# The eight-head attention layer of a graph network: four of a chunk's 64 gathers made by one-hot products on TensorE, and the end chunk in a free part of a buffer

## What is computed

```python
def _gat_conv(x, W, att_src, att_dst, bias, src, dst, heads, out_ch, concat):
    n = x.shape[0]
    h = (x @ W).reshape(n, heads, out_ch)
    a_src = jnp.einsum('nhc,hc->nh', h, att_src)
    a_dst = jnp.einsum('nhc,hc->nh', h, att_dst)
    logits = jax.nn.leaky_relu(a_src[src] + a_dst[dst], NEG_SLOPE)
    m = jax.ops.segment_max(logits, dst, num_segments=n)
    e = jnp.exp(logits - m[dst])
    denom = jax.ops.segment_sum(e, dst, num_segments=n)
    alpha = e / denom[dst]
    msgs = h[src] * alpha[:, :, None]
    out = jax.ops.segment_sum(msgs, dst, num_segments=n)
    out = out.reshape(n, heads * out_ch) if concat else out.mean(axis=1)
    return out + bias
loops = jnp.arange(N, dtype=edge_index.dtype)
src = jnp.concatenate([edge_index[0], loops])
dst = jnp.concatenate([edge_index[1], loops])
h = x @ W_map + b_map
h = _gat_conv(h, W1, att_src1, att_dst1, b1, src, dst, heads=8, out_ch=8, concat=True)
```

## Time and profile before

| | us |
|---|---|
| median of 3 runs | 3327.02 (3321.53 to 3329.48) |
| the profiled execution | 3327.11 |
| its span, first to last instruction | 3325.3 |
| the stretch of `edge_chunks`, first gather to last join | 2396.6 to 3010.8 |
| POOL, busy in the whole span | 970.5 |
| TensorE, granted clock over the span | 0.899 |

### The profile page before, as it was taken

How to read it: one execution, slowest core, us unless ns; L and a number is a source line. 1 busy time by engine, 2 the same in 40 slices (tenths; PEclk the granted TensorE clock), 3 DMA queues, 4 the chain that set the end, 5 groups by cost and what they waited for, 6 DMA issues and landing times. The chain is left out here.

```text
span 3325.3 us, 42240 instructions
## 1 busy us (share of the span) xinstructions
PE 2793.2 (84%) x14474; PEld 2097.3 (63%) x14474; DVE 1770.5 (53%) x4020; ACT 1383.9 (42%) x2629; POOL 970.5 (29%) x785
## 2 busy tenths in 40 slices
PE   5778887999996999999999999999864444456997
PEld 3445774777775877878877787785423333344775
DVE  8998657999967541121122121112664444447994
ACT  4573235999995221121111111111333333333896
POOL 6110070000001632213322222230277777750000
PEclk9999897999998999999999999999756666666999
DMA  5334442111002522212211213110211111113200
GB/s 161 137 112 151 180 163 89 41 55 70 1 1 95 197 102 86 76 58 89 94 60 70 88 65 125 60 65 7 74 31 29 29 29 29 29 20 129 80 36 20
DMA packets 73828, 252.16 MB, mean 76 GB/s; under 512 B 20459, under 2 KB 52784, under 8 KB 63920
## 3 DMA queue, kind: packets, MB, share of 16 engines
q1 hardware_dynamic: 56728, 222.19, 17.7%
q0 software_dynamic: 16896, 27.27, 3.8%
HBM read 218.24 MB, written 31.17 MB: 75 GB/s over the span
## 5 line engine op out<-in xcount | busy, mean ns | idle before, releaser
L2961 PE MATMUL psum<-gate_stream,parts 128*128 128x384 f32 (+1 forms) x3600 | 668.9, 344 | 8.6 <-ACT x L3001 4.4
L2961 PEld LDWEIGHTS psum<-gate_stream,parts 128*128 128x128 f32 x3600 | 631.6, 189 | 25.5 <-issue 6.1
L3066 POOL CAST gate_stream<-gate_adj 128x1920 fp32r<-128x1920 f16 (+1 forms) x200 | 372.2, 1868 | 836.2 <-PE psum L2961 826.4
L2321 PE MATMUL psum<-gat_h,gat_pair 128*128 128x129 f32 (+1 forms) x3750 | 571.1, 292 | 10.4 <-DVE gat_pair L2125 9.5
L2321 PEld LDWEIGHTS psum<-gat_h,gat_pair 128*128 128x128 f32 (+1 forms) x3750 | 460.9, 190 | 126.2 <-issue 77.7
L1637 POOL DMA_INDIRECT edge_rows<-edge_table,src_idx x440 | 436.4, 992 | 184.8 <-issue 133.5
L3099 DVE SCALAR_TENSOR_TENSOR gate_work<-psum,bhh,gate_work 128x384 f32<-128x384 f32 (+1 forms) x80 | 50.1, 626 | 780.8 <-PE psum L2908 763.1
L2125 DVE SCALAR_TENSOR_TENSOR gat_pair<-gat_above,gat_adj 128x512 f32<-128x512 f32 (+3 forms) x525 | 328.7, 626 | 87.4 <-PE psum L2321 58.0
L2234 ACT ACTIVATE gat_above<-psum,gat_as 128x512 f32<-128x512 f32 (+3 forms) x525 | 329.4, 627 | 42.9 <-PE psum L2309 41.2
L2225 ACT ACTIVATE psum<-gat_ad_rows,gat_as 128x512 f32<-128x512 f32 (+3 forms) x525 | 334.9, 638 | 16.9
L2080 DVE SCALAR_TENSOR_TENSOR gat_acc<-gat_adj,gat_q,gat_acc 128x512 f32<-128x512 f16 (+3 forms) x497 | 330.7, 683 | 0.0
(11 more groups left out here) (497 smaller groups left out, 3918.9 us busy)
## 6 DMA issues: line engine op xcount, KB each, us to landing
gate_adj<-adj SPq DMA_DIRECT2D x35, 2400.0 KB, 8.1
gat_adj<-adj SPq DMA_DIRECT2D x8, 3200.0 KB, 11.0
gcn_adj<-adj SPq DMA_DIRECT2D x10, 2400.0 KB, 8.5
adj<-count_stage SPq DMA_DIRECT2D x196, 100.0 KB, 1.7
gate_adj<-adj SPq DMA_DIRECT2D x5, 2800.0 KB, 9.0
edge_rows<-edge_table,src_idx POOLq DMA_INDIRECT x440, 2.5
gcn_adj<-adj SPq DMA_DIRECT2D x2, 3200.0 KB, 10.2
gcn_adj<-adj SPq DMA_DIRECT2D x2, 2800.0 KB, 10.0
```

Source lines behind the costliest of these rows:

```text
L2321: mm = e.matmul(ps[0:p, b, a:a + D + 1], pair[:, g % 2, i * P:i * P + p], h1[:, hi, h, :], start=hi == 0 and i % 3 == 0, stop=hi == NT - 1 ...
L2961: mm = e.matmul(ps[:, f, 0:hi - lo], parts[:, t, m, f, :], stream[:, (NGG * i + t // GG) % GR, 0:windows(i), t % GG * W:(t % GG + 1) * W], ...
L3066: e.tensor_copy(stream[:, n % GR, 0:windows(i), :], cols[:, i % 2, 0:windows(i), g * GW:(g + 1) * GW]).then_inc(widened, 1)
```

## The change

For the six chunks of 64 steps, the last four steps are no longer gathered by POOL (DRAWN): POOL has 60 gathers in these chunks and 416 in all. The four steps (a **batch**) come from PE. ACT and DVE first split the 72 numbers of each node into three bf16 parts (`parts`, 216 columns for a tile). A second scratch in HBM holds the source indices in f16, read back as `src_rows`. For each batch PE spreads the source indices over the partitions (`sources`), ACT copies them to f16 (`lay`), DVE compares them with the node numbers of each of the 25 tiles (`find`, ring of 12 buffers), PE adds up 4 products for each tile (`pull`, 216 columns, f16 one-hot and bf16 parts, PSUM banks 6 and 7), and DVE adds the three parts into `edge_rows` (`draw`, two reductions). The batch of chunk 0 stands ahead of all look-ups. The batch of chunk c + 1 stands among the sums of chunk c: from the fifth step on, every second `keep_busy` product gives way to the 4 products of one tile; on DVE `find` and `draw` follow the weighting of chunk c.

The end chunk uses rows 32 to 55 of side 0 and of `edge_hot`, which chunk 6 (32 steps) leaves free, and no longer waits for a chunk's sums. Every `widen` has one `keep_busy` product ahead of it. `masked`, `logit`, `top`, `part`, `fwd` and `bwd` lie in tiles that are free at that time. Clearing the banks (now L2004) stands behind the maximum's transposes (now L1994), and the small products are in bank 4 in place of bank 7. Some semaphores are merged.

```diff
+DRAWN = (4, 4, 4, 4, 4, 4, 0, 0)
+NSRC = NP // 2 - 32
+RING = 12
...
+        e.dma_start(self.k.src_scratch.rearrange("(j p q) -> p j q", j=KJ, p=KP), self.sf[:]).then_inc(self.kept, 16)
...
+        e.tensor_scalar(self.sf[:], part(0), -float(NSRC), None, ALU.add)
...
+        free_g = spare_g[:].rearrange("p t w -> p (t w)")
+        masked, logit, top = (free_g[:, n * KP * HEADS:(n + 1) * KP * HEADS].rearrange("p (s h) -> p s h", h=HEADS) for n in range(3))
+        part = spare_t[:, 0:NT * SUMS].rearrange("p (t w) -> p t w", w=SUMS)
+        fwd, bwd = (spare_t[:, NP - (n + 1) * tiles * P:NP - n * tiles * P].rearrange("p (i q) -> p i q", q=P) for n in range(2))
...
+        by_pool = [size[c] - DRAWN[c] for c in range(end + 1)]
+        batches = [(c, s) for c in range(end + 1) for s in range(by_pool[c], size[c], EG)]
+        of_chunk = [[m for m, (k, _) in enumerate(batches) if k == c] for c in range(end + 1)] + [[], []]
...
+        side = [c % 2 for c in range(end)] + [0]
+        base = [0] * end + [size[end - 1]]
+        row = lambda c: rows[:, side[c], base[c]:base[c] + size[c], :]
+        arrival = side[:end] + [2]
+        landed = [16 * sum(by_pool[k] for k in range(c + 1) if arrival[k] == arrival[c]) for c in range(end + 1)]
+        hot_of = lambda c: hot[:, base[c]:base[c] + size[c], :]
...
-                    if c >= 2:
+                    if 2 <= c < end:
                         e.wait_ge(summed, c - 1)
-                    for s in range(size[c]):
+                    for s in range(by_pool[c]):
...
+                def find(share):
+                    for m, lo, hi in share:
+                        if lo == 0:
+                            e.wait_ge(src_in, m + 1)
+                        for t in range(lo, hi):
+                            n = m * NT + t
+                            if n >= RING:
+                                e.wait_ge(pulled, n - RING + 1)
+                            e.tensor_scalar(one[:, n % RING, :], src_wide[:, m % 2, :], self.tile_ids[:, t:t + 1], None,
+                                            ALU.is_equal).then_inc(ones, 1)
+                def draw(m):
+                    c, s = batches[m]
+                    e.wait_ge(pulled, (m + 1) * NT)
+                    if 2 <= c:
+                        e.wait_ge(summed, min(c - 1, end - 2))
+                    for j in range(2):
+                        of = ps[:, 6 + j, 0:6 * ROWS].rearrange("p (s n w) -> p s w n", n=3, w=ROWS)
+                        inst = e.tensor_reduce(row(c)[:, s + 2 * j:s + 2 * j + 2, 0:ROWS], of, AX.X, ALU.add)
+                    inst.then_inc(drawn, 1)
...
+                e.wait_ge(split, 1)
+                e.tensor_tensor(part[:, :, 0:ROWS], acc[:], parts[:, :, 0, :], ALU.subtract).then_inc(begun, 1)
...
+                e.wait_ge(split, 2)
+                e.tensor_tensor(part[:, :, 0:ROWS], part[:, :, 0:ROWS], parts[:, :, 1, :], ALU.subtract).then_inc(begun, 1)
...
+                for m in of_chunk[0]:
+                    find([(m, 0, NT)])
+                    draw(m)
...
+                    for m in of_chunk[c + 1]:
+                        find([(m, 0, NT)])
+                        draw(m)
...
+                def lay(c):
+                    for m in of_chunk[c]:
+                        e.wait_ge(src_up, m + 1)
+                        if m >= 2:
+                            e.wait_ge(ones, (m - 1) * NT)
+                        e.copy(src_wide[:, m % 2, :], ps[:, 6 + m % 2, :]).then_inc(src_in, 1)
+                def near(n):
+                    if n:
+                        e.wait_ge(begun, 2 * n - 1)
+                    e.copy(parts[:, :, n, :], part[:, :, 0:ROWS] if n else acc[:]).then_inc(split, 1)
+                near(0)
+                lay(0)
+                near(1)
+                near(2)
...
                     if 0 < c < end:
+                        lay(c + 1)
                         take(c - 1)
...
+                    if c == 0:
+                        lay(1)
...
+                    self.keep_busy(e, ps[:, 6 + g % 2, :], 1)
+                    broadcast(6 + g % 2, g, self.place_rows).then_inc(wide, 1)
...
+                def sources(c):
+                    for m in of_chunk[c]:
+                        if m:
+                            e.wait_ge(drawn, m)
+                        broadcast(6 + m % 2, (first_step[c] + batches[m][1]) // EG, self.src_rows).then_inc(src_up, 1)
+                def pull(share):
+                    for m, lo, hi in share:
+                        if lo == 0:
+                            e.wait_ge(src_in, of_chunk[batches[m][0]][-1] + 1)
+                            if m:
+                                e.wait_ge(drawn, m)
+                            for b in (6, 7):
+                                e.matmul(ps[:, b, 0:6 * ROWS], zero[:, 0:P], zero[:, 0:6 * ROWS], start=True, stop=False,
+                                         skip_group_check=True)
+                        for t in range(lo, hi):
+                            e.wait_ge(ones, m * NT + t + 1)
+                            for s in range(EG):
+                                mm = e.matmul(ps[:, 6 + s // 2, (s % 2) * 3 * ROWS:(s % 2 + 1) * 3 * ROWS],
+                                              one[:, (m * NT + t) % RING, s * P:(s + 1) * P],
+                                              parts[:, t].rearrange("p n w -> p (n w)"), start=False, stop=t == NT - 1,
+                                              skip_group_check=True)
+                            mm.then_inc(pulled, 1)
...
+                    every = 2 if size[c] == KP else 1
...
+                        pulls = [(m, (s - 4) // every, (s - 4) // every + 1) for m in of_chunk[c + 1]
+                                 if s >= 4 and (s - 4) % every == 0 and (s - 4) // every < NT]
+                        pull(pulls)
+                        if not pulls and s < size[c] - 1:
+                            self.keep_busy(e, ps[:, 5, :], 1)
+                    for m in of_chunk[c + 1]:
+                        pull([(m, -(-(size[c] - 4) // every), NT)])
...
+                sources(0)
+                e.wait_ge(split, 3)
+                for m in of_chunk[0]:
+                    pull([(m, 0, NT)])
+                e.wait_ge(drawn, len(of_chunk[0]))
+                e.wait_ge(begun, 7)
+                for c in range(end + 1):
+                    look_ups(c)
+                    if c == 0:
+                        e.wait_ge(hots_t, due[0])
+                        sources(1)
                     line_up(c)
-                    if c == 0:
-                        e.wait_ge(copied, 2)
                     ends_of(c)
                     carries_of(c)
+                    peaks_of(c)
                     clear(c)
-                    peaks_of(c)
                     sums(c)
+                    if of_chunk[c + 1]:
+                        e.wait_ge(drawn, of_chunk[c + 1][-1] + 1)
+                    if of_chunk[c + 2]:
+                        sources(c + 2)
+                        e.wait_ge(src_in, of_chunk[c + 2][-1] + 1)
...
+                e.wait_ge(edges.kept, 32)
                 e.dma_start(self.place_rows[:], self.row_scratch[0:REAL * P].rearrange("(g q) -> g q", q=EG * P)).then_inc(rest, 16)
-                e.wait_ge(rest, 16 * 11)
+                e.dma_start(self.src_rows[:], self.src_scratch[0:REAL * P].rearrange("(g q) -> g q", q=EG * P)).then_inc(rest, 16)
+                e.wait_ge(rest, 16 * 12)
```

More of the change, by code:

```diff
@@ L1712, in _ @@
                     e.wait_ge(added, due[c])
-                    e.wait_ge(fetched[b], 16 * sum(size[b:c + 1:2]))
-                    e.tensor_tensor(masked[:, 0:n], rows[:, b, 0:n, 64:72], per_step(floor[:, steps(c)]), ALU.add).then_inc(masks, 1)
+                    e.wait_ge(fetched[arrival[c]], landed[c])
+                    if of_chunk[c]:
+                        e.wait_ge(drawn, of_chunk[c][-1] + 1)
+                    e.tensor_tensor(masked[:, 0:n], row(c)[:, :, 64:72], per_step(floor[:, steps(c)]), ALU.add).then_inc(logits, 1)
                     if c:
                         e.wait_ge(filled, c)
-                    e.tensor_tensor(logit[:, 0:n], rows[:, b, 0:n, 64:72], on_dst[:, steps(c), :], ALU.add).then_inc(logits, 1)
-                    e.wait_ge(logits, 2 * c + 1)
+                    e.tensor_tensor(logit[:, 0:n], row(c)[:, :, 64:72], on_dst[:, steps(c), :], ALU.add).then_inc(logits, 1)
+                    e.wait_ge(logits, 3 * c + 2)
                     e.scalar_tensor_tensor(logit[:, 0:n], logit[:, 0:n], NEG, logit[:, 0:n], ALU.mult, ALU.max).then_inc(logits, 1)
@@ L1867, in ends_of @@
                 def ends_of(c):
-                    e.wait_ge(picked, c + 1)
+                    e.wait_ge(first, 2 * c + 2)
+                    if c:
+                        e.wait_ge(taken, c)
+                    else:
+                        e.wait_ge(copied, 2)
                     e.matmul(ends[0:HEADS, :, :].rearrange("p w s -> p (w s)"), of_head[:],
```

151 lines of the change are left out of this document (74 added, 77 removed).

## The result

The changed kernel takes 3308.11 us (median of 7 runs, 3304.64 to 3311.98); the kernel before, in 7 runs beside it, 3321.53 (3319.02 to 3330.55). The ratio is 0.9951, with a 95% interval of 0.9941 to 0.9961, so the change is faster by 0.49%, 16 us (13.4 by the two medians). The forecast was 6.4 us. The time lies in the range, 1.1 us from its low end; the direction was right, the size too small by more than half. Part of the place in the range is the base: the forecast stood on 3327.0, the median of three runs before, and the seven have 3321.5.

The account below looks back on a forecast made before the run. Gathers on POOL set the pace before (83.4 us a chunk), TensorE's queue after. Chunk 5 starting 6.7 us earlier, less 0.3 in the stage ahead, nets -6.4 from 3327.11: 3320.7 us, range 3307 to 3338.

Parts of the forecast that it names:

- what is late next: From chunk 0's sums to chunk 5, look-ups behind longer sums on TensorE's queue replace the wait for gathers.
- a sign of being wrong: The prediction counts as wrong if, among other signs, a gather is waited for from chunk 2 on.
- The first comparison: Start of the stage: first look-up comparison at 2420.8 in place of 2400.17; wrong if more than 5 us off.
- from a sums' end to the next chain start: Look-ups between chunks: 20.3 us plus 1.2 for spreading sources and waiting for ACT's copy, 21.5 in all.
- the batch product: One 216-column product on PE: 0.10 us taken, lower end 0.09, upper 0.14; wrong over 0.11 or under 0.09.
- the pair of steps: Two steps with a tile among the sums: 0.90 us, including 0.40 a tile and 0.03 for the f32 load.
- S: Sums of each of chunks 0 to 4 with a batch among them: 29.5 us against 21.2; ends 27.8 and 34.
- The terms at the start: Start of the stage: added DMA, splitting, clearing, 25 tiles, `draw`, setup and `pack` sum to 21.4 us, ends 17 and 26.
- a pace of 77.7 and 18 us of cover at chunk 5: 60 gathers a chunk at 1.295 us give 77.7; TensorE's queue is late next, by 18 us.
- Weight loads in the open: Rival on batch products: 0.14 us each, 24 us more over 600 products, 3345 us; chance 0.15.
- The clock did not stay up in the look-ups: Rival claimed PE's clock stays up through the look-ups, 5 us gained plus 0.8 at `pack`: 3315 us; chance 0.18.
- The gathers did not set the pace: Rival claimed gathers still set the pace, chunk 5 starting 25 us earlier at 2867: 3302 us; chance 0.04.

Follow-up runs that it names:

- more_ones: Changed kernel, first-layer counters held at 1 or more, plus one product on ones behind each of the 25 tiles among the sums of chunks 0 to 4: 3335.0 us.
- after_again: Changed kernel with only the first layer's loaded counters held at 1 or more, one register operation each: 3319.2 us, second profile 3324.2.
- first_gathered: Changed kernel, counters held at 1 or more, chunk 0 gathered whole without a batch: 3317.5 us; measured again as first_gathered_2: 3311.5 us.
- the pair run once more: Kernel before and changed kernel, both with only the first layer's counters held at 1 or more: 3334.8 and 3319.2 us.

## Why the prediction was right, and where it fell short

**Right: the direction, and what is late next.** Gathers set the pace before, and PE's look-ups behind longer sums do after. The wait for gathers is gone from chunks 1 to 5, and more work for PE lengthens the stage. Two things were foreseen otherwise. POOL does not visibly wait for sums: ahead of chunk 2's first gather it sits idle 0.30 us, as ahead of any (1.96 in more_ones, whose sums end later). And a gather is still waited for after chunk 2, which the prediction named as a sign of being wrong: chunk 6's chain waits 6.1 us. That wait is off the path, since it ends at 2914.0 and PE is with the sums of chunk 5 until 2929.2.

**Right: most prices.** The first comparison came 23.1 us behind the identity's copy (24.4 forecast, 0.4 of it ahead of the copy), from a sums' end to the next chain start it was 21.5 (2553.95 to 2575.40; 21.5 forecast), the chain of chunks 1 to 4 26.8 (26.9), the batch product 0.09 (0.10), the pair of steps 0.86 (0.90). The comparisons, the end chunk's place and the clearing cost nothing, as said.

**Short: the sum of the terms.** The forecast had -7.1 for the stage, measured were -15.5. The 0.4 of the added DMA lies ahead of the first mark and is left out of the first row. The 8.4 us are:

| step | forecast | measured | difference |
|---|---|---|---|
| identity's copy to chunk 0's chain | 105.9 | 104.3 | -1.6 |
| sums of chunks 0 to 4 | 147.5 | 142.4 | -5.1 |
| chains and look-ups between | 235.4 | 234.8 | -0.6 |
| chunk 5 to the last copy | 108.1 | 107.0 | -1.1 |

The step that failed is S: "S = 29.5", where the rows show 28.15, 29.17, 28.0, 29.0 and 28.1. Of the 1.0 us, 25 x (0.90 - 0.864) = 0.9 is the pair of steps: the prediction had worked out 0.09 a product, saw rows of f16 products that left 0.01 to 0.03 for a load, and took 0.10 where 0.0925 shows (0.37 for four); and it added 0.03 for the f32 load behind the tile, of which 0.02 shows. The product runs 500 times among sums in sequence, so 0.0075 us of it are 3.8 us, more than half of the whole gain that was forecast. The other 2.6 us that the sum has for the lower level of the clock were right: the sums spend 5.0 us a chunk there, which costs 2.5. The terms at the start were rounded up in the same direction: clearing and 25 tiles took 12.0 us (2409.57 to 2421.59), not 13.1. The last row, 1.1, is no more than the same kernel varies there (106.7 and 107.7 in the two profiles of after_again). On the path of the changed kernel the experiments found no mechanism that the prediction lacked.

A second term was mis-sized, off the path. The prediction took 1.295 us off for each gather saved, the average with the stalls, and so a pace of 77.7 and 18 us of cover at chunk 5. Without a stall a gather takes 0.95 + 0.30 = 1.25, and the stalls under DVE's joins stay when gathers go (in each of chunks 3 to 5, before and after, one gather of 2.12 to 2.14 us and one of 2.31 or 2.32). 83.5 - 4 x 1.25 = 78.5 is the pace of first_gathered_2. With it the gathers of chunk 5 landed at 2870.3, and their cover was 11.5 us.

**The rivals.** Weight loads in the open would have made a product 0.14 us; it is 0.0925, no more than 216 columns take at the rate of the products on ones (256 in 0.11), so that a load of full-array weights lies wholly beside the product ahead of it. The Trainium skill, "TensorE: Matmul & The Clock Gate", Part 3 (The mechanism), lists that a load overlaps running products only where the row group differs; this trace disagrees, with 0.0925 us a product at the upper level of the clock, where all use the full array. The same section also says that a load into the background weight buffer is pulled ahead, and that fits the trace. The clock did not stay up in the look-ups (0.50 from 2557.40 on), and taking out the products on ones changed nothing. The gathers did not set the pace. They came to do so where chunk 0 was gathered, with four gathers more and PE's work 13 us earlier, and at chunk 5 where the comparisons read f32.

**Outside the stage.** The forecast stood on one profiled execution of before whose last part was 324.9, near the upper of the two levels; the changed kernel's profiled execution had 317.5. So -7.4 of the -19.0 between the two profiles is not the change's. Nor need the first +3.8 be: in two profiles of first_gathered the identity's copy lies 3.1 us apart. Which of the runs without a profile had which last part isn't known, but the difference of the medians, 13 us as it stands and 16 by the ratio, agrees with the stage's -15.5, and the pair run once more has 15.6 and 14.6.

## What to carry to other kernels

Where a change trades a resource for work on a queue that runs in sequence, the forecast is a small difference of large sums: a hundredth of a microsecond in the repeated product outweighed every other error here, so give its two ends the whole range and take the value that the nearest rows support, not that value with a margin. Price what is saved by what one more of it takes, not by an average that holds stalls. Ask for each batch separately what hides it: five of six lay in a wait of 14 us, and the one ahead of the first chunk lay in the open and cost 13 us of start for 5 us of gathers. Compare two profiles by stages between marks that both have; a stage that the change doesn't touch and that differs by 5 to 7 us says how far a span can be trusted.

## What the runs showed of the hardware

An instruction on DVE can hold up the issue of an indirect DMA on POOL for what is left of it, and which does it is not a matter of its length. Of a subtraction of two f32 tiles in SBUF (2.03 us) 1.87 us were left when a gather began, and it took 2.69 us in place of 0.95; of the next 1.43 were left, and the gather took 2.26. A row of 25 comparisons of f32 numbers into f16 (9.98 us) let one gather pass in 1.25 us and held the next for 8.01, to its end; 25 comparisons of f16 numbers (7.91 us) held none (0.94 to 0.95 us each). The Trainium skill, "SBUF — State Buffer", Who interferes with whom, says that an operation with both inputs in SBUF contends only with GpSimd's reads, and infers that generating descriptors needs the write side; by that inference the subtraction should not hold a gather, and here it does. A gather here takes its rows' numbers from `src_idx`, a tile in SBUF, so a read by POOL may be what is held; no run separates the two. For the f32 comparisons the trace fits the same section's rule that a mode which uses both port pairs blocks the other engine fully. That section lets such comparisons from f16 enter these modes too, and those held nothing; which mode either kind ran in, no row shows.

In a row, a comparison of 512 numbers takes 0.30 to 0.32 us from f16 and 0.40 from f32, and 0.70 where it reads PSUM. Here the source's place mattered more than its type.

The same instructions behind the stage take 317.5 or 322.5 to 325 us, in different executions of one program, by a granted clock of 0.66 or of 0.53 to 0.59 in the first 60 of the last 317.5 us.

A row of products of 216 columns, each with its own full-array f16 weights, goes at 0.0925 us a product at the upper level of the clock, with no load in the open.
